# Orders of their own for the first five and last seven steps of a two-layer graph network kernel

## The reference

```
h   = relu(layernorm(x))
# 4 attention heads: Wh = h W[hd];  f1 = Wh a[hd,:256];  f2 = Wh a[hd,256:]
# e = leakyrelu(f1 + f2^T), masked by adj; attn = softmax(e); out = elu(attn Wh)
h2  = concat(4 heads)                       # 1024 features
out = elu(one more such head(h2, W_out, a_out))   # 256 features
y   = relu(out w1 + b1) w2 + b2 + out
x   = x + layernorm(y) * gamma + beta
h   = relu(layernorm(x))
x   = x + deg * (h Wi^T + b) + adj (h Wj^T)
```

## Time and profile before

| | |
|---|---|
| median of three runs | 872.32 us (870.45 to 875.13) |
| the profiled execution | 870.21 us, of which the span from the first to the last instruction is 868.3 us |
| busy, share of the span | PE 98%, PE weight loads 90%, DVE 81%, POOL 80%, ACT 77% |
| instructions | 20346 |
| mean granted clock of PE | 0.990 of full |

### The profile page before, as it was taken

How to read it: one execution, slowest core, us unless ns; L and a number is a source line. 1 busy time by engine, 2 the same in 40 slices (tenths; PEclk the granted TensorE clock), 3 DMA queues, 4 the chain that set the end, 5 groups by cost and what they waited for, 6 DMA issues and landing times.

```text
span 868.3 us, 20346 instructions
## 1 busy us (share of the span) xinstructions
PE 849.3 (98%) x6400; PEld 785.6 (90%) x6400; DVE 701.7 (81%) x2002; ACT 668.0 (77%) x1801; POOL 693.6 (80%) x944
## 2 busy tenths in 40 slices
PE   8799999999999999999999999999999999999986
PEld 5599999999999999999999999999999999999963
DVE  5877888888888888888888888888888888877764
ACT  4789878878887887888788788778878877776642
POOL 2579888888888888888888888888888888888862
PEclk7899999999999999999999999999999999999999
DMA  6200010111110011111001111100111110000000
GB/s 197 74 13 26 26 36 3 39 37 39 37 38 27 13 37 39 38 38 38 25 15 37 37 39 37 39 20 19 37 37 37 38 38 17 10 26 26 25 25 24
DMA packets 29976, 30.46 MB, mean 35 GB/s; under 512 B 1808, under 2 KB 29472, under 8 KB 29872
## 3 DMA queue, kind: packets, MB, share of 16 engines
q1 hardware_dynamic: 29808, 29.11, 11.0%
q0 software_dynamic: 64, 0.07, 0.0%
HBM read 20.78 MB, written 8.39 MB: 34 GB/s over the span
## 4 chain that ended last, share of the span: by engine, by line
PE 94%; POOL 2%; DVE 1%; ACT 1%; issue 1%; POOLq 0%; ACTq 0%; DVEq 0%
PE ps L1222 84%; PE ps L1340 4%; PE ps L1414 2%; PE ps L1296 2%; PE ps L1395 2%; PE ps L1362 1%; PE ps L1210 1%; ACT lend L968 0%; ACT lend L957 0%; PE ps L1181 0%; DVE res L510 0%; POOL wo L425 0%; POOL lend L409 0%; POOL h_lo L375 0%; DVE lend L734 0%
## 5 line engine op out<-in xcount | busy, mean ns | idle before, releaser
L375 POOL TENSOR_TENSOR h_lo<-h2v,h_hi 128x512 fp32r<-128x512 f32 x128 | 165.1, 1291 | 49.9 <-ACT h_hi L992 49.8
L1222 PE MATMUL ps<-gh_hi,wh_hi 128*128 128x256 f32 x512 | 152.5, 298 | 1.6 <-DVE gh_lo L601 1.6
L1222 PE MATMUL ps<-wo_hi,h_hi 128*128 128x258 f32 x512 | 150.3, 294 | 0.0
L1222 PE MATMUL ps<-wo_lo,h_hi 128*128 128x258 f32 x512 | 144.4, 282 | 0.0
L1222 PE MATMUL ps<-gh_hi,wh_lo 128*128 128x256 f32 x512 | 144.3, 282 | 0.0
L1222 PE MATMUL ps<-wo_hi,h_lo 128*128 128x258 f32 x512 | 144.1, 281 | 0.0
L1222 PE MATMUL ps<-gh_lo,wh_hi 128*128 128x256 f32 x512 | 143.6, 280 | 0.0
L601 DVE TENSOR_TENSOR gh_lo<-ps,gh_hi 128x512 fp32r<-128x512 f32 x128 | 88.4, 691 | 52.4 <-ACT gh_hi L935 52.2
L646 DVE SCALAR_TENSOR_TENSOR h2v<-h2e,ps 128x512 f32<-128x512 f32 x128 | 87.7, 685 | 16.9 <-POOL h2e L381 16.8
L957 ACT ACTIVATE lend<-lend,zm 128x128 f32<-128x128 f32 x256 | 98.9, 391 | 3.0 <-DVE zm L663 3.0
L1222 PEld LDWEIGHTS ps<-wo_lo,h_hi 128*128 128x128 f32 x512 | 97.3, 190 | 4.4
(11 more groups left out here) (171 smaller groups left out, 2725.6 us busy)
## 6 DMA issues: line engine op xcount, KB each, us to landing
xa<-in_x SPq DMA_DIRECT2D x32, 256.0 KB, 3.7
xr<-in_x SPq DMA_DIRECT2D x32, 256.0 KB, 2.9
out<-res SPq DMA_DIRECT2D x32, 256.0 KB, 3.2
lend<-in_L_gnn_W_heads SPq DMA_DIRECT2D x4, 256.0 KB, 4.5
wo<-in_L_gnn_W_out SPq DMA_DIRECT2D x1, 1024.0 KB, 8.0
l1w_sb<-in_L_gnn_W SPq DMA_DIRECT2D x1, 512.0 KB, 8.0
lend<-in_L_gnn_w SPq DMA_DIRECT2D x2, 256.0 KB, 3.6
oe<-in_L_gnn_a_out SPq DMA_DIRECT2D x1, 256.0 KB, 8.9
```

The costliest lines, as they stand in the source:

```text
L375: pool.tensor_tensor(h2_lo[:, u, :, :].rearrange("p c n -> p (c n)"), h2v[u % 2][:, :], h2_hi[:, u, :, :].rearrange("p c n -> p (c n)").bi ...
L1222: return pe.matmul(out_, lhs, rhs, start=start, stop=stop)
```

## The change

- ACT's queue starts the loads of `a_rows`, the four heads' W and `adj` as its first work. SP's queue loads x of pair 0, then a new broadcast `a_bc` (rows of a for heads 2 and 3, on all partitions), x of pair 1 and the later weights.
- W a of heads 0 and 1 stays on PE; that of heads 2 and 3 becomes eight dots on DVE (`heads_dots`). PE loses `heads_transposes(2)`, `(3)` and `heads_products(2)`, `(3)`, DVE loses two copies.
- Steps 0 to 4 (`first()`) and 32 to 38 (`last()`) are written out unit by unit, in an order of their own on each engine; steps 5 to 31 keep the loop. The once-only work moves into `first()`. The numbers and places of the `warm` matmuls change with it.
- The last pair goes in halves: by feature halves from `out2` to `ffn`, by graphs from `norm2` to `store`. Its `ov_low`, `hidden_low`, `norm2`, `scale2` and `norm3` are DVE's.

The core of it:

```diff
+HEAD, TAIL = 5, 32
-            for t in range(PAIRS + STAGES - 1):
+            for t in range(HEAD, TAIL):
                 at(t // 2, t % 2)
...
-            def load_heads():
-                sp.dma_start(a_rows[:, :], ...)
-                for hd in range(H): sp.dma_start(wh[:, :, hd, :], ...)
+            def load_a_rows():
+                sp.dma_start(a_bc, a_heads[2:H].rearrange("h (j o) -> h j o", j=2).partition_broadcast(P)).then_inc(a_bc_in, 16)
+            def store_half(p, s):
+                wait_part(sp, "result_ready", p, s)
+                sp.dma_start(pair_of(out, p)[:, s, :], res[p.e][:, s, :]).then_inc(stored[p.e], 16)
+            def first():      # SP
+                load_x(pair(0)); load_a_rows(); load_x(pair(1)); load_later_weights(); load_x(pair(2)); load_x(pair(3)); load_ffn_weights()
+                load_residual(pair(0)); load_x(pair(4)); load_residual(pair(1))
...
-            pool.dma_start(adj_i[:, :], adj).then_inc(adj_in, 16)
+            def last():       # POOL, its end
+                ... hidden_low(pair(30)); add_beta(pair(30)); rstd2(pair(30))
+                out_less(pair(31), 0); out_less(pair(31), 1); scale2(pair(30)); rstd3(pair(30)); add_bias(pair(30)); add_beta(pair(31))
+                rstd2(pair(31)); add_bias(pair(31)); rstd3(pair(31))
...
+            def heads_dots(hd):
+                dve.wait_ge(heads_in[hd], 16)
+                dve.wait_ge(a_bc_in, 16)
+                for c in range(C):
+                    for j in range(2):
+                        dot(wh[:, c, hd, :], a_bc[:, hd - 2, j, :], wa[:, c, j, hd:hd + 1])
+            def normal_here(name, p, dst, src, mv, rs, done, s):
+                wait(dve, name + "_rstd", p)
+                dve.tensor_scalar(dst[p.e][:, s, :], src, mv[p.e][:, s, 0:1], rs[p.e][:, s:s + 1], ALU.subtract, ALU.mult).then_inc(S[done], 1)
+            def first():      # DVE
+                selectors(); a_cols_copy(); norm1_stats(pair(0)); norm1_var(pair(0)); norm1_stats(pair(1)); norm1_var(pair(1)); heads_t_copy(0)
+                heads_t_copy(1); heads_dots(2); adj_cast(); heads_dots(3); mask_cast(); wa_copy(); heads_low(); f_cols_split(pair(0)); out_dots(0)
+                score_mask(pair(0), 0); out_dots(1); soft_max(pair(0), 0); score_mask(pair(0), 1); out_dots(2); soft_sum(pair(0), 0)
+                soft_max(pair(0), 1); norm1_stats(pair(2)); norm1_var(pair(2)); f_cols_split(pair(1)); soft_sum(pair(0), 1); at_low(pair(0), 0)
+                adj_rows(); score_mask(pair(1), 0); gh_low(pair(0), 0); soft_max(pair(1), 0); at_low(pair(0), 1); gh_low(pair(0), 1)
+                score_mask(pair(1), 1); gh_low(pair(0), 2); gh_low(pair(0), 3); soft_sum(pair(1), 0); out_dots(3); soft_max(pair(1), 1)
+                ...
+            def last():       # DVE, its end
+                ... result(pair(28)); wh2_scores(pair(31)); rows2_copy(pair(31)); hidden_whole(pair(30)); score_mask2(pair(31))
+                soft_max2(pair(31)); h3t_low(pair(29)); soft_sum2(pair(31)); soft2(pair(31)); add_b2(pair(30)); norm2_stats(pair(30))
+                norm2_var(pair(30)); out_elu(pair(31), 0); add_mi(pair(29), 0); mj_low(pair(29), 0); out_elu(pair(31), 1); mj_low(pair(29), 1)
+                add_mi(pair(29), 1); ov_low_here(pair(31), 0); residual2(pair(30)); ov_low_here(pair(31), 1); norm3_stats(pair(30))
+                norm3_var(pair(30)); hidden_whole(pair(31), 0); hidden_whole(pair(31), 1); hidden_low_here(pair(31), 0); result(pair(29))
+                hidden_low_here(pair(31), 1); h3t_low(pair(30)); add_b2(pair(31)); norm2_stats(pair(31)); norm2_var(pair(31)); add_mi(pair(30), 0)
+                mj_low(pair(30), 0); norm2_here(pair(31), 0); norm2_here(pair(31), 1); scale2_here(pair(31), 0); mj_low(pair(30), 1)
+                scale2_here(pair(31), 1); add_mi(pair(30), 1); residual2(pair(31), 0); residual2(pair(31), 1); result(pair(30))
+                norm3_stats(pair(31), 0); norm3_stats(pair(31), 1); norm3_var(pair(31)); norm3_here(pair(31), 0); norm3_here(pair(31), 1)
+                h3t_low(pair(31), 0); h3t_low(pair(31), 1); add_mi(pair(31), 0); mj_low(pair(31), 0); mj_low(pair(31), 1); add_mi(pair(31), 1)
+                result(pair(31), 0); result(pair(31), 1)
...
+            act.dma_start(a_rows[:, :], a_heads.rearrange("h (r o) -> (h r) o", o=P)).then_inc(a_in, 16)
+            for hd in range(H):
+                act.dma_start(wh[:, :, hd, :], w_heads[hd].rearrange("(c f) o -> f c o", f=P)).then_inc(heads_in[hd], 16)
+            act.dma_start(adj_i[:, :], adj).then_inc(adj_in, 16)
+            def first():      # ACT
+                row_selectors(); norm1(pair(0)); heads_high(); ht_copy(pair(0)); norm1(pair(1)); rows_copy(pair(0)); out_high()
+                score_leaky(pair(0), 0); ht_copy(pair(1)); h_high(pair(0)); h_high(pair(1)); soft_exp(pair(0), 0); score_leaky(pair(0), 1)
+                soft_exp(pair(0), 1); at_high(pair(0), 0); rows_copy(pair(1)); norm1(pair(2)); gh_high(pair(0), 0); score_leaky(pair(1), 0)
+                at_high(pair(0), 1); gh_high(pair(0), 1); soft_exp(pair(1), 0); gh_high(pair(0), 2); gh_high(pair(0), 3); ht_copy(pair(2))
+                ...
...
+            def mixed_high(p, b):     # the matmuls of mixed that read h3_hi; waits for h3t_hi of graph b
+            def mixed_low(p, b):      # those that read h3_lo; waits for h3t_lo
+            def first():      # PE
+                warm(3, 6); a_transpose(); warm(3, 6); heads_transposes(0); heads_transposes(1); heads_products(0); heads_products(1)
+                h_transposes(pair(0)); warm(2, 6); score_cols(pair(0)); h_transposes(pair(1)); warm(2, 6); score_rows(pair(0)); scores(pair(0), 0)
+                warm(5, 6); scores(pair(0), 1); adj_transpose(); warm(2, 6); score_cols(pair(1)); warm(12, 6); prob_transposes(pair(0), 0); warm(2, 6)
+                score_rows(pair(1)); scores(pair(1), 0); gh_unit(pair(0), 0); prob_transposes(pair(0), 1); gh_unit(pair(0), 1); scores(pair(1), 1)
+                h_transposes(pair(2)); l1w_transposes(); gh_unit(pair(0), 2); gh_unit(pair(0), 3); warm(5, 6); h2_unit(pair(0), 0, 0)
+                ...
+            def last():       # PE, its end
+                ... wh2_part(pair(31), 1, 2)
+                wh2_part(pair(31), 1, 3); gather(pair(28)); hidden(pair(30), 0); hidden(pair(30), 1); ffn_out(pair(30)); score_rows2(pair(31))
+                scores2(pair(31)); warm(3, 0); h3_transposes(pair(29)); ffn(pair(30), 0); ffn(pair(30), 1); prob_transposes2(pair(31))
+                mixed(pair(29), 0); out2(pair(31), 0); out2(pair(31), 1); mixed(pair(29), 1); warm(4, 0); hidden_by_rows(pair(31), 0)
+                hidden_by_rows(pair(31), 1); gather(pair(29)); ffn_out(pair(31)); warm(2, 0); ffn_by_rows(pair(31), 0); h3_transposes(pair(30))
+                ffn_by_rows(pair(31), 1); warm(2, 0); mixed(pair(30), 0); mixed(pair(30), 1); warm(2, 0); gather(pair(30)); warm(10, 0)
+                h3_transposes(pair(31), 0); h3_transposes(pair(31), 1); mixed_high(pair(31), 0); mixed_low(pair(31), 0); mixed_high(pair(31), 1)
+                mixed_low(pair(31), 1); gather_half(pair(31), 0); warm(2, 0); gather_half(pair(31), 1)
+            first()
             steps(one)
+            last()
```

More of the change, by code:

```diff
@@ L38 @@
 STAGES = 8
+HEAD, TAIL = 5, 32
+LAST_STORES = 2
 WO = F + 2
@@ L259, in wait, with part_done, wait_part, nodes @@
                 eng.wait_ge(S[name], q.count(PER[name], PER[name] if k is None else k))
+        def part_done(name, s):
+            return first_half[name] if s == 0 and name in first_half else S[name]
+        def wait_part(eng, name, p, s):
+            if s is None:
+                wait(eng, name, p)
+            elif name in first_half:
+                if s == 0:
+                    eng.wait_ge(first_half[name], 1)
+                else:
+                    wait(eng, name, p)
+            else:
+                wait(eng, name, p, s + 1)
+        def nodes(s):
+            return slice(0, 2 * P) if s is None else slice(s * P, (s + 1) * P)
+        def halves(s, bank, banks):
+            if s is None:
+                return ps[:, bank, :].rearrange("p (c n) -> p c n", c=2)
+            return ps[:, banks[s], s * F:(s + 1) * F].unsqueeze(1)
+        def part(s):
+            return slice(0, 2) if s is None else slice(s, s + 1)
         def half(p, lag=0):
@@ L703, in hidden_whole, with ov_low_here @@
-            def hidden_whole(p):
-                wait(dve, "hidden_hi", p)
+                dve.scalar_tensor_tensor(ov[:, part(s), :], oe[:, part(s), :], 0.0,
+                                         halves(s, B_OUT, B_OUT_LAST), ALU.min, ALU.max)\
+                   .then_inc(part_done("out_elu", s), 1)
+            def ov_low_here(p, s):
+                wait_part(dve, "ov_hi", p, s)
+                dve.tensor_tensor(ov_lo[:, part(s), :], ov[:, part(s), :], ov_hi[:, part(s), :].bitcast(F32), ALU.subtract)\
+                   .then_inc(part_done("ov_lo", s), 1)
```

(27 more changed lines are left out.)

441 lines of the change are left out of this document (260 added, 181 removed).

## The result

The kernel after takes 866.49 us (median of 8 runs, 864.82 to 866.62), the kernel before 871.66 beside it: a ratio of 0.9942, 95% interval 0.9926 to 0.9958. That is 5.1 us or 0.58% faster. The forecast was 861.6, which is 10.7 us less than the 872.3 that it started from. The direction held, and the time lies at the last 0.01 us of the range; the gain is less than half of what was worked out.

The account below looks back on a forecast made before the run. PE was taken to bound the kernel from 40 to 826 us, one pair's chain at either end. Head 5.6, gather 0.5 and last chain 4.6 sum to 10.7 us off 872.3: 861.6 us, range 857.5 to 866.5.

Parts of the forecast that it names:

- The method: Whole kernel: gain is earlier first h2_unit, plus gather(28) moved, plus shorter last chain, less any new stall between.
- slower: Steps 5 to 31: they settle into another phase, each losing PE time; 877.8 us at 0.6 us a step; chance 0.05.
- The head's 5.6 us: Start of kernel: first h2_unit at 34.7 instead of 40.27 us, 5.6 us earlier, bounds 3.6 to 7.1.
- x of pair 1 at 8.5: Head: x of pair 1 lands at 8.5 us, within 5.4 to 9.0, adding 1.5 us to the early bound.
- the walk: Head: written orders followed with the old trace's durations, first h2_unit at 33.2 us if x of pair 1 comes at 7.0.
- it all shifts: Head: DVE is dense from x of pair 1 on, so its 1.5 us delay moves the first h2_unit to 34.7.
- the loads take the head's gain: Head: shared DMA engines land W, a_bc and x of pair 1 2 to 4 us later; 866.0 us; chance 0.14.
- SP's own transfers are small until 3 us: Head loads: argument against W, a_bc and x of pair 1 landing 2 to 4 us later than supposed.
- Steps 1 to 4 hold the same units: 0: Steps 1 to 4: same PE units as before, run without a gap, so no change in time.
- Between: 0, less the gather's 0.5: Up to the last wh2_part: PE full with the same units, 0, but gather(28) moves behind that end, -0.5 us.
- The last chain's 4.6 us: From the last wh2_part to the end: 37.1 instead of 41.7 us, 4.6 less, bounds 2.6 to 5.9.
- The forecast on the dots: Head: eight dots cost DVE 2.8 us for two copies removed, +1.4 net; PE loses two transposes and two product groups.

Follow-up runs that it names:

- last pair whole: Kernel after with its last steps' orders kept, the last pair whole instead of in halves (except norm2, scale2, norm3), its ReLU ahead of mixed missing: 870.07 us, ratio 0.999.
- 18 filling: Kernel after with 18 instead of 10 filling matmuls ahead of the last pair's h3_transposes: 864.87 us, ratio 0.9925.
- all in one: Kernel after with loads in order of need, mj_low(28) ahead of residual2(29), add_bias(31) and result(30) moved later, 14 filling matmuls: 862.29 us, ratio 0.9898.
- experiment 4: Kernel after with W issued by SyncE again and pair 1's statistics moved behind the dots in DVE's list: 867.77 us, ratio 0.9956.
- last steps alone: Kernel before's loads and first steps, with the kernel after's last seven steps and last pair in halves: 870.11 us, ratio 0.9988 to the kernel before.

## Why the prediction was right or wrong

The last chain by its five intervals, in us:

| | predicted | before | after | last pair whole | 18 filling | all in one |
|---|---|---|---|---|---|---|
| to the end of `out2` | 9.8 | 10.58 | 11.12 | 11.14 | 11.14 | 10.61 |
| to `add_b2` | 9.5 | 10.78 | 9.85 | 11.03 | 9.85 | 9.85 |
| to `h3_transposes` | - | 10.24 | 9.32 | 9.71 | 9.32 | 8.50 |
| to the end of `result` | - | 7.52 | 7.25 | 8.98 | 5.89 | 6.43 |
| to the end | 2.55 | 2.59 | 2.30 | 2.65 | 2.36 | 2.32 |
| sum | 37.1 | 41.71 | 39.84 | 43.51 | 38.56 | 37.71 |

(The prediction cut the two middle ones at `residual2`: 6.05 and 9.2, sum 15.25; the kernel after has 5.78 and 10.79, sum 16.57. In the last column the two halves' transposes start 1.27 us apart, and the row counts to the first.)

- **The method held.** PE has no wait over 0.2 us from 60 to 825 us, the steps keep their 25.38 us, and the lead of the first steps arrives at the last ones to 0.01 us in every kernel. The rival "slower", a new phase of the steps, did not happen.
- **The head's 5.6 us came as 3.36, and three terms of its sum failed.** "x of pair 1 at 8.5": it was there at 9.15, 0.65 us late. From there to `f_cols_split` the walk had 8.1 us (8.5 to 16.6) and the trace 8.86: the walk let DVE's list set the pace, and the last wait is for PE, which ran at half pace (eight small products take 1.85 us at 16.12 and 0.95 at 23.49). From `f_cols_split` to the first `h2_unit` the walk had 18.1 us and the trace 18.90. These are 0.65, 0.76 and 0.80 us, together 2.2. Both lengths hardly change: 8.86 us in ten of eleven profiled executions with this order on DVE (9.01 in the other), whether x came at 7.69 or at 11.22, and 18.9 us in the fourteen executions with these first steps other than experiment 4's. So "it all shifts" with x of pair 1 was the right mechanism; two thirds of the miss are in the walk over the engines and one third in the transfer.
- **The transfer of x of pair 1** was put at an issue at 2.7 and 5.8 us to landing. It was issued at 1.73 and took 7.4, more than the 6.3 of the range that the prediction took. The Trainium skill, DMA: Bandwidth & Descriptors, section "Issuing engines are not separate DMA queues", has transfers of different engines sharing the 16 DMA engines; the trace agrees (W 8.6 us to landing with `w_out` beside it, 6.8 without). The prediction weighed this rule for W alone and let the sum stand, since `heads_low` waits for DVE's list. For W that ground held: DVE takes `wh_lo` without a pause, 0.40 us after `wh_hi` is done. But x of pair 1 shared the engines as well, and holding `w_out` back brought it, and the head, 1.5 us forward. "SP's own transfers are small until 3 us" was wrong: the 1 MB of `w_out` was issued at 2.20.
- **The rival "the loads take the head's gain"** has the time nearest to the measured one, 866.0, by luck: x of pair 1 came 0.65 us later than supposed, not 2 to 4, the head gave more than its 0.5 to 2.4, and the missing rest is in the steps between and in the tail.
- **"Steps 1 to 4 hold the same units: 0"** was off by 0.7 us: each kernel with these first steps loses 0.67 to 0.75 us between the first `h2_unit` and step 6. 0.30 of it is a wait for `f_split` of pair 2 at 42.59 and 0.2 is lost at 41.0 between a group of transposes and the next product; the rest was not located.
- **"Between: 0, less the gather's 0.5"** failed by 1.15 us. PE's list shows one wait there (0.2 us, near 800). By the starts of the matmuls, 0.33 us are lost at 799.2 in front of `gather(27)`, 0.20 at 750.6 in front of a `gh_unit` and 0.13 at 795.5 in front of transposes; the rest is spread over smaller gaps. The last steps alone lose as much (1.12 us), so it is their orders; which of their moves costs it was not tried and stays open.
- **The last chain's 4.6 us came as 1.9.** Of the 2.7 missing, 1.3 is the clock (16 or 18 filling matmuls bring the chain to 38.6). 0.5 is the wait of `gather(28)`, which the prediction ran "first as before": it gave the gather its 0.47 us and did not ask whether its operand would be there. 0.8 is in the softmax: `prob_transposes2(31)` was put 7.0 us into the chain and comes at 8.4, and at 7.9 with the gather's wait gone, still behind a wait for DVE's probabilities. The other intervals are within 0.35 us and cancel. The halves themselves were sized well: 1.2 us of the way to `add_b2` where the prediction had 1.3, and 3.7 in all. Once the clock is kept, the way from `residual2` to the end of `result` takes 9.4 us, predicted 9.2.
- **The forecast on the dots** (PE spared, DVE +1.4 net) had the right sign: undoing them costs 5.5 us. The prediction gave them no price of their own.

## What to carry to other kernels

A load that is issued earlier lands earlier only if what is issued beside it can wait: list all transfers of the first microseconds with their sizes, order them by need across all queues, and hold back by a semaphore what is not needed yet. A wait for one late load costs all that stands behind it in that engine's list, so moving the load and moving its consumer in four lists are one edit. Ask of each late load what the list behind its consumer adds: here 8.86 and 18.9 us that hardly changed told that x of pair 1 and not W set the head. In a closing chain look at the granted clock after each gap in TensorE's work, and check the column against the durations of equal matmuls; a few filling matmuls up to the next real one gave 1.3 us here.
